# Layer 0's softmax sums: a detour through DRAM for the reciprocal, and the weighing of the partial contexts two steps later

## The reference, cut to what matters

```python
scores = jnp.einsum('bhnd,bhjcd->bhnjc', q, kc) / jnp.sqrt(Dh)
scores = jnp.clip(scores, -10.0, 10.0)
mask = adj_matrix.reshape(N, Nc, CHUNK)[None, None]
scores = jnp.where(mask == 0, -10.0, scores)
attn = jax.nn.softmax(scores, axis=-1)      # over each chunk of 128 keys, of which there are 8
ctx = jnp.einsum('bhnjc,bhjcd->bhnd', attn, vc)
out = ctx @ Wo.T + bo
out = layernorm(out + x) * gamma + beta
```

## Time and profile before

| | us |
|---|---|
| median of 3 runs (lowest to highest) | 2103.32 (2099.75 to 2114.32) |
| the profiled execution | 2103.01 |
| its span, first to last instruction | 2101.2 |
| mean granted TensorE clock (share of full speed) | 0.908 |
| PE busy | 1671.2 (80%) |
| DVE busy | 1600.2 (76%) |
| ACT busy | 1339.1 (64%) |

### The profile page before, as it was taken

The page is one execution under the profiler, slowest core; times in us unless marked ns, Lnnn a source line. Parts: engine busy times, 40 slices in busy tenths (PEclk is TensorE's granted clock), DMA queues, the critical chain, the costliest instruction groups (busy, mean ns, idle before and its releaser), DMA issues. The chain is left out here.

```text
span 2101.2 us, 36838 instructions
## 1 busy us (share of the span) xinstructions
PE 1671.2 (80%) x13620; PEld 1065.1 (51%) x13620; DVE 1600.2 (76%) x2710; ACT 1339.1 (64%) x1751; POOL 122.9 (6%) x130
## 2 busy tenths in 40 slices
PE   2888887878788557799989886777877757999997
PEld 1333343334333246677767665556655554455544
DVE  3676877868778745888888899888898856766664
ACT  2665656656655357667777698898888834455453
POOL 0000110100100100000000000000000000000000
PEclk9989989989999858899998998878998879999999
DMA  7545254353453131111111121112111211000000
GB/s 205 134 100 128 70 132 105 91 126 96 98 125 87 51 114 41 41 51 41 41 51 42 42 72 67 57 61 74 62 64 68 73 57 39 11 11 20 10 11 20
DMA packets 74923, 146.51 MB, mean 70 GB/s; under 512 B 11937, under 2 KB 34722, under 8 KB 74754
## 3 DMA queue, kind: packets, MB, share of 16 engines
q1 hardware_dynamic: 74754, 144.23, 24.6%
HBM read 101.85 MB, written 8.78 MB: 53 GB/s over the span
## 5 line engine op out<-in xcount | busy, mean ns | idle before, releaser
L1050 ACT ACTIVATE g<-s_all,steep_d 128x1024 fp8e4<-128x1024 f32 x608 | 642.4, 1135 | 42.9 <-PE acc L991 20.6
L991 PE MATMUL acc<-parts,g 128*128 128x102 bf16 (+1 forms) x6144 | 418.0, 229 | 27.0 <-DVE sums L1141 19.7
L991 PEld LDWEIGHTS acc<-parts,g 128*128 128x128 fp8e4 x6144 | 401.5, 99 | 60.6 <-issue 43.6
L973 PE MATMUL post<-parts,edge 128*128 128x396 bf16 (+1 forms) x1024 | 234.4, 385 | 84.9 <-DVE base L1149 84.9
L561 ACT ACTIVATE e<-s_ps 128x1024 f32<-128x1024 f32 x256 | 248.4, 1023 | 24.9 <-PE s_ps L420 18.6
L1134 DVE TENSOR_TENSOR g<-g,edge 128x1024 int32<-128x1024 int32 x192 | 227.9, 1218 | 32.6 <-ACT g L1050 32.5
L706 DVE SCALAR_TENSOR_TENSOR e<-e,bound 128x1024 f32<-128x1024 f32 x160 | 188.7, 1213 | 32.1 <-ACT e L561 30.9
L416 PE MATMUL s_ps<-qs,ks 128*128 128x512 f32 x512 | 200.3, 502 | 9.5 <-issue 7.6
L973 PEld LDWEIGHTS post<-parts,edge 128*128 128x128 fp8e4 x1024 | 102.5, 103 | 192.8 <-issue 108.7
L432 PE MATMUL sum_ps<-e,pick 128*32 128x256 f32 x2048 | 142.3, 397 | 67.5 <-DVE e L703 39.4
L567 ACT ACTIVATE chunk<-ctx_ps 128x512 f32<-128x512 f32 x128 | 76.3, 596 | 171.0 <-PE ctx_ps L441 171.0
(11 more groups left out here) (152 smaller groups left out, 2149.9 us busy)
## 6 DMA issues: line engine op xcount, KB each, us to landing
s_all<-s_rows SPq DMA_DIRECT2D x96, 512.0 KB, 3.7
inv_all<-inv_rows SPq DMA_DIRECT2D x256, 128.0 KB, 2.8
qs<-split SPq DMA_DIRECT2D x128, 128.0 KB, 3.2
ks<-split SPq DMA_DIRECT2D x128, 128.0 KB, 2.4
x<-in_x SPq DMA_DIRECT2D x8, 512.0 KB, 6.8
inv_rows<-inv SPq DMA_DIRECT2D x32, 128.0 KB, 1.7
adj_in<-in_adj SPq DMA_DIRECT2D x8, 512.0 KB, 4.1
out_x<-x SPq DMA_DIRECT2D x8, 512.0 KB, 3.2
```

The lines of the kernel that those rows point to most:

```text
L973: ins = pe.matmul(self.post[:, it % 2, 0:H * 3 * W1].rearrange("p (h k c) -> p h k c", h=H, k=3), self.c.edge[:, jt, it * P:(it + 1) * P], ...
L991: ins = pe.matmul(self.acc[:, bank, o:o + self.NS], self.g[:, h % RING, jt, it * P:(it + 1) * P], self.upper[par][:, jt, h, :, :].rearrang ...
L1050: act.activation(self.g[:, h % RING, jt, :], self.s_all[:, h % 2, :], ACT.Relu, bias=self.steep_d[par][:, jt, h:h + 1], scale=STEEP, satur ...
```

## The change

Layer 0 alone. The sums of a group are copied by ACT from PSUM into SBUF (`copy_sums`, 128x256, after the exponentials of the steps 0, 4, 8, 12), which is what PE now waits for before the next group's sums. SP stores the copy to DRAM, waits, and loads only the used rows back with four DMAs, in a form of 128x64. DVE takes the reciprocal of that 128x64 tile in SBUF, in the steps 2, 6, 10 and 14. SP stores the inverses and loads them broadcast, as before. The weighing moves to the steps 9, 11, 13, 15 (half 0) and the next stage's 1, 3, 5, 7 (half 1).

```diff
-    FIRST_HALF, SECOND_HALF = (7, 9, 11, 13), (15, 1, 4, 6)
+    FIRST_HALF, SECOND_HALF = (9, 11, 13, 15), (1, 3, 5, 7)
...
-        inv = sb("inv", [P, QUARTER])
-        inv_dram = nc.dram_tensor("inv_rows", (2, 2, H, DH, QUARTER), F32, kind="Internal").ap()
+        sum_rows, inv = sb("sum_rows", [P, QUARTER]), sb("inv", [P, QUARTER // 4])
+        sum_dram = nc.dram_tensor("sums_dram", (2, 2, H, DH, QUARTER), F32, kind="Internal").ap()
+        inv_dram = nc.dram_tensor("inv_rows", (2, 2, H, 2 * GROUP, QUARTER), F32, kind="Internal").ap()
...
             def inverses(b, half, group):
                 m = 2 * b + half
                 n = 2 * m + group
+                wait_apart(c, sp, sums_copied, n + 1)
+                sp.dma_start(sum_dram[half, group].rearrange("h r n -> (h r) n"), sum_rows[:, :]).then_inc(sums_stored, 16)
+                wait_apart(c, sp, sums_stored, 16 * n + 16)
+                for h in range(H):
+                    sp.dma_start(inv[h * DH:(h + 1) * DH, :],
+                                 sum_dram[half, group, h, 0:2 * GROUP, :].rearrange("r (k n) -> (r k) n", k=4)).then_inc(
+                                     sums_loaded, 16)
                 wait_apart(c, sp, inverted, n + 1)
-                sp.dma_start(inv_dram[half, group].rearrange("h r n -> (h r) n"), inv[:, :]).then_inc(inv_stored, 16)
+                sp.dma_start(inv_dram[half, group].rearrange("h r (k n) -> (h r k) n", k=4), inv[:, :]).then_inc(inv_stored, 16)
                 wait_apart(c, sp, inv_stored, 16 * n + 16)
                 for p in (2 * group, 2 * group + 1):
                     wait_apart(c, sp, pair_weighed, 4 * m + p + 3)
...
                 if jt % GROUP == 0 and not (isinstance(b, int) and b == 0 and i == 0):
-                    pe.wait_ge(inverted, 4 * b + i // GROUP)
+                    pe.wait_ge(sums_copied, 4 * b + i // GROUP)
...
+            def copy_sums(n):
+                act.wait_ge(summed, GROUP * n + GROUP)
+                if not (isinstance(n, int) and n == 0):
+                    act.wait_ge(sums_stored, 16 * n)
+                act.activation(sum_rows[:, :], sum_ps, ACT.Copy).then_inc(sums_copied, 1)
...
                     exps(b, i, 0)
                     exps(b, i, 1)
+                    if i % GROUP == 0 and not (first and i == 0):
+                        copy_sums(4 * b + i // GROUP - 1)
...
-            def invert(b, half, group):
-                n = 4 * b + 2 * half + group
-                dve.wait_ge(summed, GROUP * n + GROUP)
-                if not (isinstance(n, int) and n == 0):
-                    dve.wait_ge(inv_stored, 16 * n)
-                dve.reciprocal(inv[:, :], sum_ps).then_inc(inverted, 1)
+            def invert(n):
+                dve.wait_ge(sums_loaded, 64 * n + 64)
+                dve.reciprocal(inv[:, :], inv[:, :]).then_inc(inverted, 1)
...
                     clip(b, i, 0)
-                    if i == 8:
-                        invert(b, 0, 1)
-                    elif i in (4, 12):
-                        invert(b, i // T, 0)
-                    elif i == 0 and not first:
-                        invert(b - 1, 1, 1)
+                    if i % GROUP == 2 and not (first and i == 2):
+                        invert(4 * b + i // GROUP - 1)
                     clip(b, i, 1)
...
             def tail():
-                invert(B - 1, 1, 1)
+                weigh(B, 1)
                 update(B - 2, 1)
-                weigh(B, 1)
                 residual(B - 1, 1, 0, False)
-                weigh(B, 4)
-                weigh(B, 6)
+                weigh(B, 3)
                 update(B - 1, 0)
+                invert(4 * B - 1)
+                weigh(B, 5)
+                weigh(B, 7)
                 residual(B - 1, 1, 1, False)
                 update(B - 1, 1)
```

More of the change, by code:

```diff
@@ L246, in layer0 @@
             c.sem(k) for k in ("summed", "inverted", "inv_stored", "chunk_copied", "pair_weighed", "added", "ctx_ready"))
+        sums_copied, sums_stored, sums_loaded = c.sem("sums_copied"), c.sem("sums_stored"), c.sem("sums_loaded")
         inv_loaded = [c.sem("inv_loaded_a"), c.sem("inv_loaded_b")]
@@ L311, in inverses @@
                     for h in range(H):
-                        rows = inv_dram[half, group, h, 0:2 * GROUP, :].rearrange("(q j) n -> q j n", q=2)[:, j:j + 2, :]
+                        rows = inv_dram[half, group, h].rearrange("(q j) n -> q j n", q=2)[:, j:j + 2, :]
                         sp.dma_start(inv_all[h * DH:(h + 1) * DH, p % 2, :, :],
@@ L599, in tail @@
                 copy_chunk(B - 1, STEPS - 1)
+                copy_sums(4 * B - 1)
                 normed(B - 2, 1)
@@ L707, in clip @@
                                          op1=ALU.min).then_inc(p_ready, 1)
-            def invert(b, half, group):
-                n = 4 * b + 2 * half + group
-                dve.wait_ge(summed, GROUP * n + GROUP)
-                if not (isinstance(n, int) and n == 0):
-                    dve.wait_ge(inv_stored, 16 * n)
-                dve.reciprocal(inv[:, :], sum_ps).then_inc(inverted, 1)
+            def invert(n):
+                dve.wait_ge(sums_loaded, 64 * n + 64)
+                dve.reciprocal(inv[:, :], inv[:, :]).then_inc(inverted, 1)
             def weigh(b, i):
                 half, p = pair_at(i)
-                m = 2 * b + half - (0 if i >= 7 else 2)
+                m = 2 * b + half - (0 if i >= 9 else 2)
                 dve.wait_ge(inv_loaded[p % 2], 64 * (2 * m + p // 2 + 1))
@@ L769, in stage @@
                 for i in range(STEPS):
-                    if first and i == 7:
+                    if first and i == 9:
                         dve.wait_ge(const_stored, 48)
-                    if i in FIRST_HALF or i in SECOND_HALF and not (first and i < 7):
+                    if i % 2 == 1 and not (first and i < 9):
                         weigh(b, i)
                     clip(b, i, 0)
-                    if i == 8:
-                        invert(b, 0, 1)
-                    elif i in (4, 12):
-                        invert(b, i // T, 0)
-                    elif i == 0 and not first:
-                        invert(b - 1, 1, 1)
+                    if i % GROUP == 2 and not (first and i == 2):
+                        invert(4 * b + i // GROUP - 1)
                     clip(b, i, 1)
```

## The result

| | before | after |
|---|---|---|
| median of 6 runs, us | 2107.3 (2099.8 to 2114.3) | 2159.6 (2157.6 to 2165.0) |
| ratio, 95% interval | | 1.025 (1.0226 to 1.0275) |
| span of the profiled execution | 2101.2 | 2155.8 |
| end of layer 0 in it | 734.2 | 792.1 |
| DVE busy in layer 0 | 531.6 | 496.7 |

The account below looks back on a forecast made before the run. It took the q stack's wait in SP's queue and the DMA chain to bound layer 0, no engine being full. First stage 5.5, six cycles 51, last stage 3 and tail 9.5 added 69 to 2103: 2172 us (2133 to 2197).

Parts of the forecast that it names:

- What bounds: Layer 0: no engine is full; ACT's k split waits 72.9 us for the q stack, in cycles of 84.9 us.
- The q stack behind reciprocal and weighing: SP's queue: stack waits for step 10's reciprocal and step 11's weighing, starting at 58.4 us against 50.1 after the chain.
- Step 14: Sums' hop replaces the inverses' hop in the DMA chain, second clip and residual behind it; chain +0.2 us (0 to +1).
- the landing of the four small loads: Loads of the sums in SP's queue: 2.2 us from last issue, between nothing and 3 us, with no row showing it.
- DVE's relief: DVE, chain's end to step 10's reciprocal: three reciprocals, 5.25 us out and 1.65 in; 47.5 busy plus 5 idle.
- last sign of being wrong: DVE's list of waits: the prediction is wrong if waits other than the two it named show there.
- TensorE's clock: PE around the k split: longer stall costs clock, +2 us a cycle, 12 in all, not priced in the sum.
- Rival B: Clock or PE sets the pace from step 14 on: 2184 us, or 2200 with more idle; chance 0.16.
- Both ends: Layer 0 outside the six cycles: first stage +5.5 us, last stage +3, tail +9.5.
- C: DVE's relief comes through whole, the q stack not being what a cycle waits for: 2074 us; chance 0.06.
- D: Effects cancel, no idle left in the stretch and cheap ends: 2120 us, needing 7 us a cycle less; chance 0.08.
- twice the idle: Upper case for DVE's stretch before the q stack, doubling the 5 us of idle taken: +11.5 us a cycle.

Follow-up runs that it names:

- e3: Changed kernel with the q stack issued in SP's queue between the loads of the sums and the inverses' store of half 0 group 1; 2110.8 us.
- e4: Changed kernel with q stack and k stack each issued between the loads of the sums and the store of the inverses in SP's queue; 2078.1 us.
- e9: Kernel before with a separate buffer for k's split, only two of five mask bounds made and used; 2076.4 us.
- e2: Changed kernel with the weighing back in its old steps, keeping the detour of the sums and the small reciprocals; 2217.4 us.
- e7: Kernel before with reciprocals over only 64 of 256 columns, the other inverses left at a constant; 2090.9 us.
- e11: Kernel before with late weighing, no detour, and the q stack ahead of all of half 0 group 1 in SP's queue; 2062.1 us.
- e1: Kernel before with only the weighing moved to the later steps, full reciprocals and no detour; 2120.3 us.

## Why the prediction held, point by point

Forecast 2172 (2133 to 2197), slower; measured 2159.6. That is +69 forecast against +52 by the medians and +54.6 between the profiled executions, of which the part behind layer 0 gives back 3.3. The 57.9 us more in layer 0 come in three parts: +7.9 up to the first k split (forecast 5.5), +37.6 in six cycles (51), +12.4 from the last k split to the end (12.5). Each is the time of k splits of after, 114.06 and 661.38 us, and the end 792.1, against the earlier trace rows.

**What bounds: right.** e3 and e4 move nothing but the order of issues and take the loss away and more. e9 takes the wait itself away and shortens the cycle of before by 4.1 us; it leaves part of the mask out, but not of the instructions in the loop.

**The q stack behind reciprocal and weighing: right, and its size nearly.** From the end of the chain (reciprocal of step 14) to the q stack's start: 55.8, 58.8, 61.6, 59.4, 59.9 and 57.6 us, mean 58.9; forecast 58.4. In the third stage the weighing of step 11 had ended at 277.4 and the stack started at 280.93 behind the eight loads: the reciprocal decides, as the prediction had it, and e2 confirms it. But I compared with 50.1 us, one stage's value; the six of before average 51.1. The step that was mis-sized is this: +7.8 a cycle and not +8.3.

**Step 14: right in kind, 1.5 us too dear.** The new wait is there in all seven stages, and clip and residual follow it. From the k split to the reciprocal's end the chain takes 19.4 us on average (19.0 to 19.8); from the k split to the weighing of step 15 it took 20.7 before (20.1 to 21.3), seven stages each. So -1.3 a cycle instead of +0.2. The largest term at fault is the landing of the four small loads, for which no row stood: I took 2.2 us from the last issue. A load lands 1.6 us after its own issue (median); from the end of the fourth issue (311.27) to the reciprocal (312.45) it is 1.2 us in the third stage and 1.3 on average, so 0.9 of the 1.5 us. Most of the rest is the store of the sums with its wait, 2.3 us on average where the store of the inverses took 2.7 before. With 7.8 - 1.3 = 6.5, the measured 6.3 a cycle is accounted for; over the same six cycles both times the chain gives 1.4, and the q stack from issue to k split 0.1 less than before.

**DVE's relief: right sum, partly by luck.** I had 3.6 us a cycle come off for three reciprocals, and put back only 1.4 us of idle, because PE would be as full. From the end of the chain to the end of the reciprocal of step 10, DVE is busy 46.7 us and idle 6.1 on average, where the sum had 47.5 and 5: 52.9 against 52.5. So the work did come off as counted, and the idle I had too low; the first cycle, with only 43.6 us busy, hides half of the difference (the other five average 53.3). What the idle is I had not said. Over layer 0 DVE waits 60.1 us ahead of its clips for ACT's exponentials, against 34.2 before, and e7, which has only the relief, shows the same (61.1): 1.0 us a cycle comes through in its profile, 16 us of 38 by its runs. The prediction's last sign of being wrong, other waits in DVE's list, is met in this row, which it did not foresee.

**TensorE's clock.** PE stands idle between the q stack and the k split, and the clock falls, more than before in layer 0 as a whole: 0.87 against 0.92.

```profile
280.93:293.75 12.82, 1.56 (x19) 0.52 (x17) 0.01 (x1) 0.00 (x1) 0.00 (x0) 0.71 0.95 188
293.75:313.00 19.25, 15.27 (x105) 8.72 (x105) 9.08 (x10) 12.26 (x15) 0.00 (x0) 0.84 0.53 118
313.00:374.60 61.60, 55.59 (x433) 24.60 (x433) 53.19 (x89) 38.78 (x57) 8.35 (x7) 0.92 0.27 74
```

In the q stack's 12.8 us PE is busy 1.6 us and the clock averages 0.71, so part of it is at 1.2 GHz; but the part from the k split to the reciprocal of step 14 runs at 0.84, where the earlier trace rows has 0.82. Rival B's price was for that part, and it did not come: it takes 19.3 us against 20.6 in the third stage, and the last thing waited for in it is a DMA (6.13 us of idle ahead of the reciprocal). The stretch behind is at 0.92 here against 0.97 in the third stage of before, but that stage is the highest: the six stretches of before lie between 0.90 and 0.97, those of after, up to the reciprocal of step 10, between 0.90 and 0.95. No run here prices what the clock costs in them, and it stays open.

**Both ends.** From the last k split to the first of the last three updates of x (712.61 before, 760.85 after) it takes 2.7 us more than before, where I had 3 for the last stage; from there to the end it takes 9.7 more, where I had 9.5 for the tail. The last reciprocal and the weighing behind it, rows of DVE:

```profile
769.59 0.55 DVE L729 RECIPROCAL inv<-inv 128x64 f32<-128x64 f32 x1
776.07 1.23 DVE L740 TENSOR_TENSOR weighed<-chunk,inv_all 128x1024 f32<-128x1024 f32 x1 [5.93 <-DMA inv_all<-inv_rows]
```

From the reciprocal's end to the first weighing 5.9 us, as in the sum (722.0 to 727.9). The first stage was 2.4 us dearer than forecast.

**The rivals.** C needed the q stack not to matter; it starts 11 us after its data. D needed 7 us a cycle less than forecast; there were 2.2.

**A slip in the range.** With twice the idle, 10 us for 5, the sum gives +13.5 a cycle and not +11.5, and with no idle +3.5 and not +3.3, so six cycles span 21 to 81 us and not 20 to 69. The measured 37.6 lies in both.

## What to carry to other kernels

A DMA queue is a program of its own: before making an operation cheaper by a detour through DRAM, list what stands behind each new wait in the queue that issues it, and when that is needed. Here the order of issues was worth some 80 us in the changed kernel, and 36 us less of DVE work, tried alone, 16. Moving a consumer later paid here only when the slack was spent (e11 against e1), by letting what is urgent go ahead of what is not; and a queue on another engine takes away the order, but the transfers still met: a stack DMA took 5.1 us to land beside the broadcasts.

## What the runs showed of the hardware

On SP's queue, a load of 8 KB in rows of 256 bytes from DRAM took 1.6 us from issue to landing (median; 1.4 to 3.2), against 2.9 for a 128 KB broadcast; a store of 32 KB in such rows took 1.5. The Trainium skill, "DMA: Bandwidth & Descriptors", section "Anatomy of one DMA", puts the fixed cost of one DMA at about 2.0 us, as a fit for the GpSimd path; on SP's queue, which is another path, the small loads' least and median, 1.4 and 1.6 us, are below it. Sixteen DMAs of 128 KB took about 8.1 us to issue from GpSimd's queue and 10 to 11 from SP's. The 128x64 reciprocal took 547 ns in SBUF and 554 from PSUM (e7), and the 128x256 one from PSUM 1754: here the width sets the price, and not where the tile lies.
